# One Trainium2 core, a coupled-oscillator integrator: tanh values as the stationary operand in four column strips, the coupling matrix streamed, outputs in two chunks

## What is computed

```python
def _derivative(q, p, drive, coupling, bias):
    i_couple = jnp.tanh(q) @ coupling.T
    dq = q - q ** 3 / 3.0 - p + drive + i_couple + bias
    dp = EPSILON * (q + ALPHA - BETA * p)
    return (dq, dp)
def _rk4_step(q, p, drive, coupling, bias):
    dq1, dp1 = _derivative(q, p, drive, coupling, bias)
    dq2, dp2 = _derivative(q + 0.5 * DT * dq1, p + 0.5 * DT * dp1, drive, coupling, bias)
    dq3, dp3 = _derivative(q + 0.5 * DT * dq2, p + 0.5 * DT * dp2, drive, coupling, bias)
    dq4, dp4 = _derivative(q + DT * dq3, p + DT * dp3, drive, coupling, bias)
    q_next = q + DT / 6.0 * (dq1 + 2 * dq2 + 2 * dq3 + dq4)
...
    return (q_next, p_next)
```

## Time and profile before

| | |
|---|---|
| median of 3 runs | 7105.63 us (7096.97 to 7106.37) |
| span of the profiled execution | 7093.8 us |
| median less that span | 11.8 us |
| integrator loop in that execution | 499.0 us to the end |
| TensorE busy, matmul and weight load | 7014.5 us (99%), 6766.4 us (95%) |
| VectorE busy | 6327.0 us (89%) |
| ScalarE busy | 3301.9 us (47%) |
| granted TensorE clock, mean | 0.997 |

### The profile page before, as it was taken

How to read it: one execution, slowest core, us unless ns; L and a number is a source line. 1 busy time by engine, 2 the same in 40 slices (tenths; PEclk the granted TensorE clock), 3 DMA queues, 4 the chain that set the end, 5 groups by cost and what they waited for, 6 DMA issues and landing times.

```text
span 7093.8 us, 600592 instructions
## 1 busy us (share of the span) xinstructions
PE 7014.5 (99%) x263499; PEld 6766.4 (95%) x263499; DVE 6327.0 (89%) x41259; ACT 3301.9 (47%) x18673; POOL 5.6 (0%) x16
## 2 busy tenths in 40 slices
PE   8889999999999999999999999999999999999999
PEld 3349999999999999999999999999999999999999
DVE  5459999999999999999999999999999999999999
ACT  3234444444444444444444444444444444444444
POOL 0000000000000000000000000000000000000000
PEclk9999999999999999999999999999999999999999
DMA  4000000000000000000000000000000000000000
GB/s 176 38 13 0 0 6 0 6 0 6 0 0 6 0 6 0 6 0 0 6 0 6 0 6 0 0 6 0 6 0 6 0 0 6 0 6 0 6 0 6
DMA packets 11596, 57.04 MB, mean 8 GB/s; under 512 B 2616, under 2 KB 2616, under 8 KB 8512
## 3 DMA queue, kind: packets, MB, share of 16 engines
q1 hardware_dynamic: 11056, 55.84, 2.0%
q10 hardware_dynamic: 528, 1.05, 0.0%
HBM read 40.11 MB, written 16.78 MB: 8 GB/s over the span
## 4 chain that ended last, share of the span: by engine, by line
PE 98%; DVE 1%; issue 0%; DMA 0%; ACT 0%; SPq 0%; DVEq 0%; ACTq 0%
PE ps L561 93%; PE ps L474 2%; PE ps L442 1%; PE ps L460 1%; PE ps L494 1%; PE ps L483 1%; DVE drive L585 0%; DMA drive<-in_coupling_t 0%; DVE neg_max L599 0%; DVE coup L696 0%; ACT head_t L349 0%; PE ps L508 0%; ACT probs L360 0%; DVE probs_t L609 0%; DVE k_aug L585 0%
## 5 line engine op out<-in xcount | busy, mean ns | idle before, releaser
L561 PEld LDWEIGHTS ps<-tanh_parts,coup 128*128 128x128 f16 x262144 | 6588.4, 96 | 5.0 <-DVE tanh_parts L585 5.0
L561 PE MATMUL ps<-tanh_parts,coup 128*128 128x32 f16 x262144 | 6588.5, 176 | 4.1 <-DVE tanh_parts L585 4.1
L585 DVE SCALAR_TENSOR_TENSOR xb<-ps,step_scale,xb 128x16 f32<-128x16 f32 (+2 forms) x16384 | 3173.6, 229 | 434.1 <-PE ps L561 363.2
L388 ACT ACTIVATE xb<-xb 128x16 f32<-128x16 f32 (+2 forms) x8196 | 1631.9, 216 | 3361.3 <-DVE xb L585 3347.7
L585 DVE SCALAR_TENSOR_TENSOR xb<-xb 128x64 f32<-128x64 f32 x9730 | 2042.6, 219 | 17.5
L394 ACT ACTIVATE tanh_parts<-xb 128x16 f16<-128x16 f32 (+2 forms) x8196 | 1573.7, 209 | 81.0
L585 DVE SCALAR_TENSOR_TENSOR tanh_parts<-xb,tanh_parts 128x16 f16<-128x16 f32 (+2 forms) x8196 | 1370.4, 172 | 0.4 <-ACT tanh_parts L394 0.4
L754 DVE SCALAR_TENSOR_TENSOR xb<-xb 128x64 f32<-128x64 f32 x2048 | 458.5, 224 | 60.1
L415 ACT ACTIVATE xb<-xb 128x64 f32<-128x64 f32 x1536 | 368.2, 240 | 0.0
L785 DVE TENSOR_TENSOR xb<-xb 128x64 f32<-128x64 f32 x1024 | 221.8, 217 | 0.0
L585 DVE SCALAR_TENSOR_TENSOR drive<-ps,row_scale,drive 128x512 f32 (+1 forms) x64 | 84.1, 1349 | 80.8 <-PE ps L483 79.4
(11 more groups left out here) (64 smaller groups left out, 780.3 us busy)
## 6 DMA issues: line engine op xcount, KB each, us to landing
xb<-in_x SPq DMA_DIRECT2D x8, 2048.0 KB, 7.9
drive<-in_x_pt SPq DMA_DIRECT2D x8, 2048.0 KB, 25.3
out_pt<-drive SPq DMA_DIRECT2D x16, 1024.0 KB, 4.3
drive<-in_coupling_t SPq DMA_DIRECT2D x8, 512.0 KB, 11.6
mask_v<-in_cond SPq DMA_DIRECT2D x8, 132.0 KB
probs<-in_wo ACTq DMA_DIRECT2D x1, 1024.0 KB, 5.9
w_qkv<-in_wq SPq DMA_DIRECT2D x1, 64.0 KB, 4.0
w_qkv<-in_wk SPq DMA_DIRECT2D x1, 64.0 KB, 5.5
```

Source lines behind the costliest of these rows:

```text
L388: nc.scalar.activation(cols(tanh_sb, CHUNKS[j]), cols(q, CHUNKS[j]), ACT.Tanh)\
L561: last = nc.tensor.matmul(ps[:, NCH * (s % 2) + j, col:col + MOVING], coup[:, k, part, P * n:P * (n + 1)], tanh_parts[:, s % 2, k, :],   s ...
L585: return V.scalar_tensor_tensor(out=out, in0=a, scalar=factor, in1=c, op0=ALU.mult, op1=op1)
```

## The change

The factors change places. `tanh_parts[:, s % 2, k, :]`, now 16 columns wide, is the stationary operand, and `coup` is streamed. The 128 columns of the TensorE array are used as four strips of 32: strip g holds the same 16 columns of tanh and gets the units 32g to 32g+31 of every output block, so `coup` is laid out as [input block, part, strip, output block, 32]. The result of strip g lies in PSUM on partitions 32g to 32g+15, batch and part on the partitions and units on the columns. VectorE's 32 x 32 block transposition (`turn_product`) turns it into `turned_sums` in SBUF, from which `add_high` and `add_low` now read. The high and low parts of tanh come out as separate rows, the parts of the coupling are summed in PSUM as before.

There are two chunks in place of four, of 3 and 5 blocks, so matmuls stream 96 or 160 columns. ScalarE's and VectorE's instructions in a stage are merged and put in another order. The scaling of the coupling writes strip by strip, 32 instructions each on ScalarE and VectorE in place of 8. The first memset is over four PSUM banks in place of `tanh_parts`.

```diff
-CHUNKS = [(0, 1), (1, 3), (3, 6), (6, 8)]
+CHUNKS = [(0, 3), (3, 8)]
...
+ORDER = [(0, 0), (0, 1), (1, 0), (1, 1)]
...
-        coup = sb("coup", [P, NC, PARTS, N], F16)
+        coup = sb("coup", [P, NC, PARTS, STRIPS, NC, SQ], F16)
...
-        tanh_parts = sb("tanh_parts", [P, 2, NC, MOVING], F16)
+        tanh_parts = sb("tanh_parts", [P, 2, NC, ROWS], F16)
+
+        turned_sums = sb("turned_sums", [P, NC, SQ])
...
             for c in range(NC):
-                nc.scalar.activation(coup[:, c, 0, :], coup_stage(c), ACT.Copy,
-                                     scale=coup_scale[:, 0:1]).then_inc(coup_high, 1)
+                for g in range(STRIPS):
+                    last = nc.scalar.activation(coup[:, c, 0, g, :, :], coup_strip(c, g), ACT.Copy,
+                                                scale=coup_scale[:, 0:1])
+                last.then_inc(coup_high, 1)
...
-                    tanh(q, 0, made)
-                    tanh(q, 1, made)
-                    split_high(parity, 0, made)
-                    split_high(parity, 1, made)
-                    tanh(q, 2, made)
-                    split_high(parity, 2, made)
-                    tanh(q, 3, made)
+                    for j in range(NCH):
+                        tanh(q, j, made)
+                        split_high(parity, j, made)
...
-                        for n in range(n0, n1):
-                            col = MOVING * (n - n0)
-                            for k in range(*CHUNKS[kj]):
-                                for part in range(PARTS):
+                        for k in range(*CHUNKS[kj]):
+                            for part in range(PARTS):
+                                for g in range(STRIPS):
                                     last = nc.tensor.matmul(
-                                        ps[:, NCH * (s % 2) + j, col:col + MOVING],
-                                        coup[:, k, part, P * n:P * (n + 1)],
+                                        product(s, j)[SQ * g:SQ * g + ROWS, :],
                                         tanh_parts[:, s % 2, k, :],
+                                        coup[:, k, part, g, n0:n1, :].rearrange("p c i -> p (c i)"),
                                         start=not begun[j],
                                         stop=(left[j] == 0 and k == CHUNKS[kj][1] - 1 and part == PARTS - 1),
-                                        skip_group_check=True)
+                                        tile_position=(0, SQ * g), skip_group_check=True)
...
+            def turn_product(s, j, now):
+
+                dve.wait_ge(product_done[j], now)
+                V.transpose(turned_sums[:, CHUNKS[j][0]:CHUNKS[j][1], :].rearrange("p c r -> p (c r)"),
+                            product(s, j)).then_inc(product_turned[j], 1)
+
             def add_high(s, j, now):
 
                 if j == 0:
 
                     dve.wait_ge(base_ready, now)
-                dve.wait_ge(product_done[j], now)
-                axpy(by_block(half_sum, CHUNKS[j]), product(s, j, 0), step_scale[:, s:s + 1],
+                dve.wait_ge(product_turned[j], now)
+                axpy(by_block(half_sum, CHUNKS[j]), turned_sum(j, 0), step_scale[:, s:s + 1],
                      by_block(base, CHUNKS[j])).then_inc(half_ready[j], 1)
...
+                turn_product(s, 0, now)
                 add_high(s, 0, now)
+                add_low(s, 0, now)
...
+                turn_product(s, 1, now)
...
                 add_high(s, 1, now)
...
+                split_low(parity, 0, made)
                 add_low(s, 1, now)
...
-                split_low(parity, 2, made)
+                split_low(parity, 1, made)
```

More of the change, by code:

```diff
@@ L218, in build @@
         product_done = [sem(f"product_done{j}") for j in range(NCH)]
+        product_turned = [sem(f"product_turned{j}") for j in range(NCH)]
         half_ready = [sem(f"half_ready{j}") for j in range(NCH)]
@@ L241, in by_block, with product, turned_sum @@
             return cols(t, blocks).rearrange("p (c b) -> p c b", b=B)
-        def product(stage, j, part):
+        def product(stage, j):
             w = CHUNKS[j][1] - CHUNKS[j][0]
-            return ps[:, NCH * (stage % 2) + j, 0:w * MOVING].rearrange(
-                "p (c m) -> p c m", m=MOVING)[:, :, B * part:B * (part + 1)]
+            return ps[:, NCH * (stage % 2) + j, 0:w * SQ]
+        def turned_sum(j, part):
+            return turned_sums[:, CHUNKS[j][0]:CHUNKS[j][1], B * part:B * (part + 1)]
         def tanh_part(parity, j, part):
@@ L695, in _ @@
                 dve.wait_ge(coup_high, c + 1)
-                V.scalar_tensor_tensor(out=coup[:, c, 1, :], in0=coup_stage(c), scalar=coup_scale[:, 0:1],
-                                       in1=coup[:, c, 0, :], op0=ALU.mult, op1=ALU.subtract)\
-                 .then_inc(coup_low, 1)
+                for g in range(STRIPS):
+                    last = V.scalar_tensor_tensor(out=coup[:, c, 1, g, :, :], in0=coup_strip(c, g),
+                                                  scalar=coup_scale[:, 0:1], in1=coup[:, c, 0, g, :, :],
+                                                  op0=ALU.mult, op1=ALU.subtract)
+                last.then_inc(coup_low, 1)
             attend(0, True)
@@ L740, in add_low @@
                 out = q_st[s + 1] if s + 1 < STAGES else q_raw
-                axpy(by_block(out, CHUNKS[j]), product(s, j, 1), step_scale[:, s:s + 1],
+                axpy(by_block(out, CHUNKS[j]), turned_sum(j, 1), step_scale[:, s:s + 1],
                      by_block(half_sum, CHUNKS[j])).then_inc(q_next[j], 1)
@@ L866, in stage @@
                 parity = (s + 1) % 2
+                made = after(now)
                 if s == 2:
@@ L870, in stage @@
                     p_sum_q3()
+                turn_product(s, 0, now)
                 add_high(s, 0, now)
+                add_low(s, 0, now)
+                if s == 0:
+                    g0_of()
+                if s == 1:
+                    rise_of(1)
+                if s == 2:
+                    q_sum_r2()
+                if s == 3:
+                    p_next()
+                turn_product(s, 1, now)
+                if s == 0:
+                    y_of()
+                if s == 1:
+                    p_sum_g0()
+                if s == 2:
+                    p_sum_r(2)
+                if s == 3:
+                    look_ahead((now + STAGES) * (COLS // STAGES))
+                    steps_done = steps_until(now)
                 add_high(s, 1, now)
[L873 removed]
+                if s == 2:
+                    z_without_last(now)
+                split_low(parity, 0, made)
                 add_low(s, 1, now)
                 if s == 0:
[L876 to L894 removed]
                     z_of_second()
+                    y_less_g0()
                 if s == 1:
                     z_of_third()
[L898 to L906 removed]
                     q_sum_r1()
@@ L923, in stage @@
                     z_of_first()
-                    split_low(parity, 3, made)
                     cubic_of(0, steps_done)
```

42 lines of the change are left out of this document (8 added, 34 removed).

## The result

The changed kernel takes 7524.2 us (median of 4 runs, 7523.7 to 7525.1), the kernel before 7106.0 in the same session. The ratio is 1.059, with a 95% interval of 1.057 to 1.060. It is slower by 5.9%; the prediction was 6955 us.

A forecast was written before the change was run, and what follows sets the result against it. The kernel before was taken as bound by TensorE's pair rate, the changed one by a latency ring: 2048 x 3.14 us saves 157 in the loop, 6 more ahead of it, so 7105.6 - 151 = 6955 us; range 6800 to 8720.

The forecast's parts named there:

- The ring: Dependent chain of each loop stage: product, transposition, adds, tanh, split, product; taken to last 3.14 us a stage.
- (1, 0): Matmuls of input chunk 1 for output chunk 0: ten quartets, putting the next last start 0.41 us after TensorE starts.
- filler: Independent VectorE instruction between the second add of chunk 0 and the second transposition; next start taken 0.11 us after the add's.
- the price of the adds: VectorE's adds in the loop, now reading SBUF: 0.18 us for 24 columns and 0.195 for 40.
- Strips at once: TensorE's four strips run together, so a quartet costs 42.5 ns at 96 columns, 69 at 160; 1.78 us a stage.
- issue: Rival: each TensorE pair keeps its 25.1 ns though on another strip, a quartet 100 ns; 8690 us, chance 0.17.
- turns: Rival: TensorE's strips run one after another, 7.14 us a stage, 15150 us; chance 0.04.
- something between: Rival: TensorE quartets of 50 to 80 ns, 3.21 to 3.51 us a stage, 7100 to 7710 us; chance 0.14.
- The clock: TensorE's granted clock, taken to stay at 2.4 GHz; rival that it falls: 4.07 us a stage, 8860 us, chance 0.04.
- The transposition's price: VectorE's transpositions: 0.27 and 0.335 us for 96 and 160 columns; rival of twice per column, 7510 us, chance 0.05.
- The double wait: VectorE's first add of a stage waits for two semaphores; 0.11 us taken for that step.
- The other stages: In the third stage two more VectorE instructions stand ahead of chunk 1's second add: 0.12 us, 0.03 on average.

The follow-up runs named there:

- e1: Changed kernel with the four adds' factor written into the instruction in place of read from memory: 7009.0 us, ratio 0.987 to the kernel before.
- e2: Changed kernel with adds reading columns of turned_sums side by side in place of 8 of every 32, values not the product's: 7527 us in one run.
- e3: Kernel before the change with its adds' factor written into the instruction: 7095.5 us in one run, beside 7096.3 for the kernel before on that chip.
- e6: Changed kernel with all four matmuls of a quartet on strip 0, values not the product's: 17263 us in one run.
- e7: Changed kernel with chunks of 1 and 7 blocks in place of 3 and 5, so quartets stream 32 or 224 columns: 8519 us in one run.
- e5: Changed kernel with the two semaphore waits of the first add in the other order: 7359.6 us, ratio 1.036 to the kernel before.
- e4: Changed kernel with the coupling stationary again and 16 columns of tanh streamed, two chunks and transpositions kept, values not the product's: 9617 us in one run.
- e10: Changed kernel with the coupling stationary again and 32 columns of tanh streamed, 16 of them zeros, two chunks and transpositions kept: 9248 us in one run.

## Why the prediction was wrong

The ring, as the prediction put it and as the timeline above has it, in us after the start of the last matmul of (1, 0), which is 0.26 ahead of the transposition:

| start of | predicted | measured |
|---|---|---|
| transposition 0 | 0.24 | 0.26 |
| `add_high` 0 | 0.62 | 0.66 |
| `add_low` 0 | 0.835 | 0.94 |
| filler | 0.945 | 1.10 |
| transposition 1 | 1.075 | 1.23 |
| `add_high` 1 | 1.445 | 1.61 |
| `add_low` 1 | 1.675 | 1.91 |
| tanh of chunk 1 | 1.905 | 2.20 |
| fp16 copy | 2.17 | 2.47 |
| remainder of chunk 1 | 2.435 | 2.74 |
| TensorE, (1, 0) | 2.69 | 2.99 |
| last matmul of (1, 0) | 3.10 | 3.38 |

The step that failed is the price of the adds: "Adds now read SBUF. 24 columns take 0.18 us". That price came from the remainders, whose factor is a number in the instruction. The adds of the kernel before, which read theirs from memory, stood in the same group at 240 ns for 24 columns, and I put the difference down to PSUM without a row that separates the two. The name of the row, `xb<-ps,step_scale,xb`, says what else differed. Three links with an add in them came out longer by 0.06 to 0.07 and the step from `add_low` 0 to the filler by 0.05: 0.25 of the 0.28 us by which the ring was short. e1 gave back 0.25 a stage. e2 and e3 took the other two reasons away. The rest of the mechanism, a ring of these instructions in this order, was right.

The rest, point by point:
- Strips at once: right, at 42.5 and 69 ns a quartet; e6 shows the alternative. The rivals of issue, turns and something between are out. The row on overlapping loads pointed that way. By the Trainium skill ("TensorE: Matmul & The Clock Gate", Part 3) starts in different tiles are about 4 ns apart, and the starts inside the changed kernel's quartets, 2 to 5 ns, agree; the 8.3 ns of e7's later quartets do not. The about 60 cycles a matmul of the Trainium skill ("TensorEngine Tiling (Array Packing)", Performance Considerations) hold for each strip by e7, not for the engine.
- The clock stayed at 1.00: right. The transposition's price: right within 0.01 us. So was its place: VectorE's queue holds the second one, TensorE does not.
- The double wait: 0.11 taken. It is on the ring and e5 removed 0.08 of it.
- The other stages: 0.04 us on average over the 3.38, against 0.03. Ahead of the loop: 5.6 us against 6.
- Sum: 2048 x (3.427 - 3.14) = 588 us, where the kernel is 569 above the forecast. What lies outside the loop was taken 17 us too long, 523 against 7524.2 - 7017.7 = 506.5. A run's time is only 1.8 us above its own span (7524.2 and 7522.3); by that the execution of the kernel before that was profiled took about 7095.6, as its fastest runs do, and 10 of the 11.8 us between its span and the median are the distance from a fast run to the median. And its loop lasts 7093.8 - 499.0 = 6594.8 us, where the forecast took TensorE's busy 6588.3.

The prediction did say that 0.074 us in the ring would turn the sign. But the 0.44 that it gave to slower went nearly all to TensorE, the clock and the transposition, and none of it to the adds, which occur four times on the ring and had no row of their own kind in SBUF. That the measured time lies inside the stated 6800 to 8720 us is luck: the range was that wide for the rival of issue, which is out.

## What to carry to other kernels

When a covered instruction moves onto the path, price it from a row with the same operands, a factor from memory included, and not from one with the same shape. Leaving a rate bound for a latency ring is only worth it if each link has been looked at: here an operand (0.20 to 0.25 us a stage), the order of two waits (0.08) and the order on VectorE (0.10 to 0.15) were worth more together than the 0.20 that separated the kernels. A thin stationary operand in four column strips does run its matmuls at once, so the swap is worth trying where TensorE is the bound; what hiding the transposition would give no run here shows.

## What the runs showed of the hardware

- A per-partition factor read from memory costs a VectorE instruction of 8 to 40 columns 0.06 us (0.244 against 0.184 at 24 columns) and a ScalarE one 0.09 (0.314 against 0.223).
- Reading 24 columns from PSUM costs a VectorE add nothing over SBUF (0.179 us in e3 against 0.184 in e1).
- The 25 ns from one 32-column matmul to the next in the kernel before are paid by four strips at once: quartets of e7 start 25 ns apart, eight times. From the ninth on matmuls on all strips together start 8.3 ns apart, 33 ns a quartet.
- e4 sat at a granted clock of 0.50 (1.2 GHz) through its loop, with TensorE busy 3.58 us of 4.47 on 16-column matmuls. e10 had 0.94 with as much of its time busy on 32 columns, and the changed kernel 1.00 at 63% and 96 or 160 columns. What decides it was not settled here.
- Of two semaphore waits in front of a VectorE instruction, the one written last costs 0.08 us when it is the later to be met (e5).
